# Attention and feed-forward layer on one core: the order within a step, and the one-hot transposed once and spread by 10-row products

## What is computed

```python
x = x + attention(layernorm(x), ctx, mask) @ Wo + bo
h = layernorm(x)                              # feed-forward input
x_mixed = k[0]*h[s-1] + k[1]*h[s] + k[2]*h[s+1]
hid    = einsum('bsd,pdm->bspm', x_mixed, W1) + b1       # 9 paths of 64
paths  = einsum('bspm,pmd->bspd', hid, W2) + b2
idx    = argmax(tanh(x_mixed @ Wo1 + bo1) @ Wo2 + bo2)
out    = x + layernorm(h + paths[idx]) * gamma + beta
```

## Time and profile before

| | us |
|---|---|
| median of 3 runs | 399.33 |
| the runs | 394.64, 399.33, 399.48 |
| profiled execution, device time | 401.61 |
| its span, first to last instruction | 399.80 |
| PE busy / DVE / POOL / ACT | 342.2 / 276.9 / 186.4 / 166.2 |
| mean granted TensorE clock | 0.948 |

### The profile page before, as it was taken

The page is one execution under the profiler, slowest core; times in us unless marked ns, Lnnn a source line. Parts: engine busy times, 40 slices in busy tenths (PEclk is TensorE's granted clock), DMA queues, the critical chain, the costliest instruction groups (busy, mean ns, idle before and its releaser), DMA issues.

```text
span 399.8 us, 7445 instructions
## 1 busy us (share of the span) xinstructions
PE 342.2 (86%) x2764; PEld 249.4 (62%) x2764; DVE 276.9 (69%) x622; ACT 166.2 (42%) x253; POOL 186.4 (47%) x217
## 2 busy tenths in 40 slices
PE   1587894896999999898999989898999899989990
PEld 0564472373567956686566857694678477866890
DVE  3346288488387849877489838985777854787866
ACT  1432543524545355434545364434651445137500
POOL 0240103201809169542939187735963397249124
PEclk9995997997899999899999999999999899989996
DMA  7308102000020002100120002000100010001003
GB/s 218 126 0 194 27 2 65 3 0 2 0 68 2 0 2 67 56 0 0 52 66 0 0 32 86 0 0 2 54 2 0 1 54 2 0 2 52 2 2 105
DMA packets 20420, 13.45 MB, mean 34 GB/s; under 512 B 10081, under 2 KB 20138, under 8 KB 20394
## 3 DMA queue, kind: packets, MB, share of 16 engines
q1 hardware_dynamic: 18754, 12.53, 10.6%
q10 hardware_dynamic: 1640, 0.57, 0.6%
HBM read 8.90 MB, written 4.19 MB: 33 GB/s over the span
## 4 chain that ended last, share of the span: by engine, by line
PE 44%; DVE 21%; issue 14%; POOL 11%; DMA 5%; ACT 4%; ACTq 1%; DVEq 0%; POOLq 0%; SPq 0%
PE ps L419 8%; PE ps L572 4%; DVE mx L1077 4%; DVE st L1024 4%; PE ps L424 3%; DMA xin<-in_x 3%; PE ps L637 3%; PE ps L527 3%; POOL x1b L1390 3%; PE ps L655 3%; POOL x L1384 2%; PE ps L660 2%; PE ps L656 2%; DMA bqs<-in_L_xattn_bq 2%; DVE osb L1095 2%
## 5 line engine op out<-in xcount | busy, mean ns | idle before, releaser
L1370 POOL TENSOR_TENSOR rs<-ve,halfneg 128x4 f32<-128x4 f32 x24 | 25.2, 1050 | 157.0 <-DVE ve L1040 157.0
L823 ACT ACTIVATE e<-ps 128x1024 f32<-128x1024 f32 x32 | 31.1, 1022 | 37.8 <-PE ps L534 37.8
L1071 DVE CAST qr<-q 128x512 fp32r<-128x512 f32 x16 | 9.4, 598 | 45.7 <-ACT q L811 45.6
L1077 DVE TENSOR_REDUCE mx<-ps 128x16 f32<-128x1024 f32 x32 | 37.8, 1210 | 0.7 <-PE ps L502 0.7
L655 PE MATMUL ps<-w2h,hmh 128*128 128x256 f32 (+1 forms) x140 | 35.8, 291 | 0.0
L656 PE MATMUL ps<-w2l,hmh 128*128 128x256 f32 (+1 forms) x140 | 34.6, 282 | 0.0
L572 PE MATMUL ps<-wo,osb 128*128 128x256 f32 x128 | 32.9, 404 | 1.6 <-DVE osb L1095 1.6
L419 PE MATMUL ps<-xmh,w1h 128*128 128x512 f32 x80 | 28.8, 443 | 6.2 <-ACT hs L867 3.9
L1421 POOL TENSOR_TENSOR hml<-hs,hmh 128x512 fp32r<-128x512 f32 x24 | 30.0, 1274 | 1.8 <-ACT hmh L877 1.7
L867 ACT ACTIVATE hs<-ps,b1s 128x512 f32<-128x512 f32 x28 | 19.4, 692 | 27.2 <-PE ps L424 27.1
L1384 POOL TENSOR_TENSOR x<-xin,bos 128x256 f32<-128x256 f32 x32 | 28.3, 914 | 0.7 <-POOL x1b L1390 0.3
(11 more groups left out here) (154 smaller groups left out, 822.1 us busy)
## 6 DMA issues: line engine op xcount, KB each, us to landing
xin<-in_x SPq DMA_DIRECT2D x8, 512.0 KB, 3.7
out<-y SPq DMA_DIRECT2D x7, 512.0 KB, 2.9
min_<-in_mask_Bx1xSxS_ik SPq DMA_DIRECT2D x8, 128.0 KB, 3.6
cst<-in_constants SPq DMA_DIRECT2D x1, 660.5 KB, 10.8
hs<-in_L_ffn_W SPq DMA_DIRECT2D x2, 288.0 KB
hs<-in_L_ffn_W SPq DMA_DIRECT2D x1, 512.0 KB
out<-xin SPq DMA_DIRECT2D x2, 256.0 KB, 2.2
cst<-in_constants SPq DMA_DIRECT2D x1, 384.0 KB, 5.7
```

What stands on the lines that cost most here:

```text
L823: nc.scalar.activation(e[:, 2 * i:2 * i + 2, :], ps[:, bank:bank + 2, :], ACT.Exp).then_inc(s_e, 1)
L1077: v.tensor_reduce(mx[:, k, :].rearrange("p (a h) -> p a h", a=2), ps[:, bank:bank + 2, :].rearrange("p a (h s) -> p a h s", s=SK), AX.X, A ...
L1370: g.tensor_tensor(ln[7][:, :], ln[6][:, :], halfneg[:, :], ALU.pow).then_inc(s_r, 1)
```

## The change

The order in a step, by engine:

- PE: `w1(0)` comes ahead of `wq` (it came after `scores_transposed(1)`). `rep(0)` comes behind `spread` (it came ahead); in its old place stands the transpose of the one-hot.
- ACT: exponentials 0 and 1, `hidden(0)`, `q_copy`, exponential 2, `hidden(4)`, exponential 3, `hidden(1)`, then `mixed_hi`, `pv_copy`, `hidden(2)`, `hidden(3)`, the copy of the transposed one-hot.
- DVE: the mix comes ahead of `q_round`, and `layernorm1_stats` of `after` ahead of `invert`. In `last_column` the wait for POOL's low part of the early mix stands one instruction earlier.

The one-hot: `oh` (128 rows by 10 columns, four tiles) is transposed by four PE transposes into 10 partitions by 512, copied by ACT to `ohT`, and each `rep(m)` is one product of 10 rows by 512 columns with a constant 0/1 matrix, `path_rows`. That matrix adds 320 columns (160 KB) to the third load of constants. There is one more use of the feed-forward banks (`NU` 14 for 13, `NFA` 6 for 5).

```diff
-C_N = C_IO + NPATH
+C_R = C_IO + NPATH + 1
+C_N = C_R + NM * P // 2
...
-        NFA, NFV, NU = NM, NM + 3, 2 * NM + 3
+        NFA, NFV, NU = NM + 1, NM + 3, 2 * NM + 4
...
+            def onehot_transposed(b, j, L=usual):
+                o = take_slot(b, j, "ohT", L)[0:NPATH + 1, 0:CH // 2].bitcast(BF16)
+                pe.wait_ge(s_oh, at(b, NJ, j + 1))
+                for k in range(NT):
+                    mm = nc.tensor.transpose(o[:, k * P:(k + 1) * P], oh[:, k, :], ident_b[:, :])
+                mm.then_inc(L.s_f, 1)
+
             def rep(b, j, m, L=usual):
                 o = take_slot(b, j, f"rep{m}", L)
                 if m == 0:
-                    pe.wait_ge(s_oh, at(b, NJ, j + 1))
...
+                    pe.wait_ge(L.s_fa, L.read_by_act(b, j, NFA))
+                r = rows_of(m)
+                nc.tensor.matmul(o[0:r, :], path_rows[0:NPATH + 1, m * P:m * P + r], ohT[0:NPATH + 1, :],
+                                 start=True, stop=True).then_inc(L.s_f, 1)
...
                 if n:
                     scores_transposed(*n, 0, front)
+                if f:
+                    w1(*f, 0)
                 if front:
                     wq(*front, fb)
                 if n:
                     scores_transposed(*n, 1, front)
                 if f:
-                    w1(*f, 0)
                     w1(*f, 4)
...
                     w1(*f, 3)
-                    rep(*f, 0)
+                    onehot_transposed(*f)
...
                 if n:
                     spread(*n)
                 if f:
+                    rep(*f, 0)
                     rep(*f, 1)
...
+            def onehot_copy(b, j, L=usual):
+                act.wait_ge(L.s_f, L.filled(b, j, "ohT"))
+                nc.scalar.activation(ohT[0:NPATH + 1, :], ps[0:NPATH + 1, L.bank(j, "ohT"), 0:CH // 2].bitcast(BF16),
+                                     ACT.Copy).then_inc(L.s_fa, 1)
...
                 dve.wait_ge(s_xm, at(b, NJ * KD, KD))
+                dve.wait_ge(s_earlyl, at(b, KD, KD))
                 v.tensor_copy(xmh[:, :, col], xm[:, :, col]).then_inc(s_xmh, KD)
                 dve.wait_ge(s_xmh, at(b, NJ * KD, KD))
-                dve.wait_ge(s_earlyl, at(b, KD, KD))
...
-                if front:
-                    q_round(*front)
                 if f and f[1] == 0:
                     second_mix(f[0])
                 if f and n[1] == NJ - 1:
                     early_mix(n[0])
+                if front:
+                    q_round(*front)
                 if f:
                     argmax(*f)
-                if n:
-                    invert(*n)
                 if after and f:
                     layernorm1_stats(*after)
+                if n:
+                    invert(*n)
```

More of the change, by code:

```diff
@@ L91, in constants @@
     c[:, C_IO:C_IO + NPATH] = np.arange(NPATH) - NPATH
+    col = np.arange(NM * P)[None, :]
+    path = np.where(col < 4 * P + DM, col // DM, col - 4 * P - DM)
+    c[:, C_R:C_R + NM * P // 2] = as_bf16((r == path) & (r < NPATH))
     return c
@@ L755, in _ @@
             w1(*f0, 3)
+            onehot_transposed(*f0)
+            w1(*f1, 4, last)
             rep(*f0, 0)
             rep(*f0, 1)
-            w1(*f1, 4, last)
             rep(*f0, 2)
@@ L766, in _ @@
             w1(*f1, 3, last)
+            onehot_transposed(*f1, last)
             for m in range(NM):
@@ L816, in maxima, with softmax_exp @@
                 nc.scalar.activation(nmT[:, :], bf16_bank(bank), ACT.Copy).then_inc(s_nT, 1)
-            def softmax_exp(b, j):
-                act.wait_ge(s_dn, at(b, NJ, j))
-                for i in range(4):
+            def softmax_exp(b, j, quarters):
+                if quarters[0] == 0:
+                    act.wait_ge(s_dn, at(b, NJ, j))
+                for i in quarters:
                     act.wait_ge(s_st, at(b, NJ * NPAIR, j * NPAIR + 2 * i + 2))
@@ L880, in step @@
                 if n:
-                    softmax_exp(*n)
+                    softmax_exp(*n, (0, 1))
+                if f:
+                    hidden(*f, 0)
                 if front:
                     q_copy(*front, 0 if f else 6)
+                if n:
+                    softmax_exp(*n, (2,))
                 if f:
-                    hidden(*f, 0)
                     hidden(*f, 4)
+                if n:
+                    softmax_exp(*n, (3,))
                 if f:
                     hidden(*f, 1)
+                if f and f[1] == 0:
+                    mixed_hi(f[0], 1)
+                if f and n[1] == NJ - 1:
+                    early_mixed_hi(n[0])
                 if n:
@@ L893, in step @@
                     hidden(*f, 3)
[L894 to L897, removed]
+                    onehot_copy(*f)
                 if f:
@@ L941, in _ @@
             hidden(*f0, 3)
+            onehot_copy(*f0)
             keep_xh2(*f0)
+            hidden(*f1, 4, last)
             selected_hi(*f0, 0)
-            hidden(*f1, 4, last)
             selected_hi(*f0, 1)
@@ L952, in _ @@
             hidden(*f1, 3, last)
+            onehot_copy(*f1, last)
             for m in range(NM):
@@ L1231, in step @@
                     early_mix(n[0])
+                if front:
+                    q_round(*front)
                 if f:
                     argmax(*f)
+                if after and f:
+                    layernorm1_stats(*after)
                 if n:
                     invert(*n)
-                if after and f:
-                    layernorm1_stats(*after)
                 if f:
```

25 lines of the change are left out of this document (8 added, 17 removed).

## The result

| | before | after |
|---|---|---|
| median, us (4 runs each) | 399.4 | 422.84 |
| range, us | 394.64 to 400.51 | 422.18 to 425.35 |
| profiled execution / its span | 401.61 / 399.80 | 422.2 / 420.4 |
| mean granted clock | 0.948 | 0.914 |

The changed kernel is slower: ratio 1.062, 95% interval 1.056 to 1.069. The forecast was 409.5, with a range up to 416: the direction was right, the time lies outside.

What follows compares the result with a forecast made beforehand. The prediction took the load of x, not PE, as the bound. Its terms, 0.4 + 3.4 + 11.9 - 1.8 - 2.6 - 0.9 = +10.4 us, gave 409.7 on the median; forecast 409.5, range 399 to 416.

Steps and rivals of the forecast that it cites:

- its 204.2 and 6: Three steps waiting for x: PE reaches `spread` near 204.2 us, then stands idle for 6 us.
- PE gains about 1.0 us a step: One-hot products on PE: 2.66 us of `rep` replaced by 1.65 us of transposes and 10-row products.
- no cheaper: Rival: 10-row products at 0.54 us each gain nothing, +0.8 in seven places, 415; chance counted with the slower case.
- The clock term: `spread`, `rep(0)` and some scores run slow after PE's idle wait: +1.9 us a step, between 0 and 3.6.
- stays low longer: Rival: the low clock lasts through the output projection, 3 x 1.7 us more, 415; chance 0.11.
- The dip in (1,1): Step (1,1) of the profiled run before: a clock dip made one projection 1.6 us longer, so 1.6 was taken off.
- The start: Steps ahead of (1,0): larger load of constants, +0.4 us; interleaved exponentials counted only as filling idle time.
- (1,0): `w1(0)` waits for the last mixed column, +2.0 us net; low clock +1.3; with smaller terms +3.4.
- (1,1): Step waiting for x: +4.5 us from order and clock, less 1.6 for the profiled run's dip.
- (3,0): Step without a wait for x: both fills -1.9 us, later `rep(0)` and `select(0)` +1.0, cheaper `rep` -1.0; in all -1.8.
- (3,1): `w1(0)` fills PE's 1.20 us idle on the exponential; POOL's low parts limit the gain to -2.6 us.
- The tail: Exposed transpose and copy (0.4 + 0.7 us) given back by cheaper `rep`; W2 starts 0.9 us sooner.

Runs made afterwards that it cites:

- h3: d1 with each 10-row product issued three times instead of once; 415.8 us, ratio 1.039.
- h1: The changed kernel without its one-hot half: all its new orders, but the 40 small products of before; 416.51 us, ratio 1.039.
- g2: The kernel before with the changed order in (3,0) and (3,1) alone and the old small products; 395.16 us, ratio 0.993.
- h2: The kernel before with only the mix, and its copies on ACT, moved ahead (on DVE ahead of `q_round`); 401.12 us, ratio 1.004.
- d2: a1 with `w1(0)` back behind the second half of the scores in (1,0) and (2,0); 407.33 us, ratio 1.026.
- a1: The changed kernel with `invert` ahead of `layernorm1_stats` again on DVE; 413.05 us, ratio 1.033.
- d1: The kernel before with only the one-hot half (transposed one-hot, 10-row products) and the places it needs; 407.36 us, ratio 1.025.
- f1: d1 with each 10-row product issued twice into the same bank; 412.73 us, ratio 1.034.
- a2: The changed kernel with exponentials 2 and 3 ahead of `q_copy` on ACT; 420.37 us, ratio 1.050.
- b1: The kernel before with only `layernorm1_stats` moved ahead of `invert` on DVE; 411.35 us, ratio 1.028.

## Why the prediction was right or wrong

- **What bounds the kernel** was read rightly: the load of x, not PE. The statistics ahead of the reciprocal cost 11.6 to 11.8 us in three steps, 11.3 by the forecast's terms; the earlier trace rows gave it. PE's idle time came as 5.03, 5.49 and 5.15 us and not 6: the terms of the prediction add up to 204.7 and 5.5, not to its 204.2 and 6.
- **"PE gains about 1.0 us a step"**, the cheaper `rep` taken off in every step, is the step that failed. The cost of one product was sized well: 0.22 us from one to the next in h3, against 0.25 taken (and 215.7 ns in the Trainium skill, "TensorE: Matmul & The Clock Gate", section "Wait — 56ns, not 53.3ns?", which this trace agrees with). A low clock behind the products was not in the sum. Beside h1, the one-hot half adds 1.7 us in (2,0), 1.6 in (2,1) and 1.6 in the tail, 6.0 in the span. The forecast's own terms of this half come to about +0.3: 1.0 for the later `rep(0)` and `select(0)` less 0.8 to 1.0 for the cheaper `rep` leaves 0.1 or 0.2 in five steps, the constants add 0.4, the tail takes 0.9 off. That is 5.7 of the missing 10.2 us. For the order alone the forecast then has about 10.1 and h1 shows 14.6 (414.4 against 399.8); 3.4 of these 4.5 are the start and 0.9 are (1,0). The rival "no cheaper" named the right edit with the wrong mechanism.
- **The clock term** of 1.9 a step was right for `spread`: 3.66, 3.62 and 3.79 us where 2.05 is full speed, so 1.6 to 1.7 and a little behind it. The slow projection, which the term had only as its upper bound and the rival "stays low longer" as a continuation of the same low clock, is a second fall: the clock was at 1.00 between the two. The dip in (1,1) that the prediction called the profiled run's own is of this kind as well, and it comes again in (1,1) of g2 and h2.
- **The start** (+3.5 against +0.4). The constants cost nothing: the first scores stand at 37.56 us after, 37.80 before. The step that failed is that exponentials interleaved with `q_copy` "fill" something and cost nothing: the copy's own wait, for the scores that still read q, was not followed. That was 3.1 of the 10.2 us by which the sum was short.
- **(1,0)** (+4.6 against +3.4): the mechanism was right, the wait for the last column 3.15 us instead of 2.8, and the products behind it slow until 112; d2 gives 4.2 back. The prediction did not follow the wait in `last_column` that the change moved.
- **(1,1)** (+2.8 against +2.9), **(3,0)** (-1.5 against -1.8) and **(3,1)** (-2.4 against -2.6): right, (1,1) with luck, since its projection stayed fast (1.99) where those of (2,0) and (2,1) did not.
- **The tail** (+1.4 against -0.9): taken as given back, the transpose and copy were not; PE waits 0.96 us on the copy and runs slow behind it. With the old products it is 51.79, -0.2.

The shortfall adds up: 3.1 + 1.2 - 0.1 + 1.6 + 1.6 + 0.3 + 0.2 + 2.3 = 10.2. Left open: why the clock is low in some steps and kernels and not in others with the same work there, as in (3,1), 36.27 in a1 and 33.58 after, and with it how much of the 6.0 us is due to the ten rows and how much to where the products stand. Whether the second fall in the kernel after would go with wider products was not tried on that kernel, only on d1.

## What to carry to other kernels

Before an instruction is moved ahead on an in-order engine, follow every wait of the moved one, not only of what it passes: the large losses of order here, the statistics and `q_copy`, are waits that were taken along to the front. Fewer TensorE instructions are not less time if the clock is low behind those that remain: price what follows at both clocks, and measure such an edit alone. And an order that pays in the steps without a late load can be kept for those steps only, which was the one gain to be had.

## What the hardware showed

- Behind 10-row products TensorE's projection took 3.68 us where 1.99 is full speed (in h3 and in d1 the granted clock was 0.53 over such a stretch, so 1.2 GHz for most of it), without idle time: in (2,0) of h3 the engine had been at work from 206.17 to 211.50. With 128-row products among them, as many columns as in f1, it took 1.99 in five steps of six. It is no rule for 10-row products alone: behind the old products and idle times of 0.81 and 0.72 us it took 3.57 in (1,1) of the kernel before, and 1.99 behind the same in (2,1). The Trainium skill ("TensorE: Matmul & The Clock Gate", section "HAM oscillation — how this bites in real kernels") tells of idle gaps; these rows show a fall with none.
- Idle times near 5 us were followed by a slow `spread` each time (six of six in after and h1). Of 2.5 to 4.1 us there are both kinds: 3.01 and 2.47 us in a2 were followed by 2.05 us, 4.11 in a2 and 3.90 in b1 by 3.78, 3.76 in b1 by 2.55.
